# Self-attention stage: the denominators' ones matmuls replaced by sums on GpSimd, with a ring of three banks

## What is computed

```
xn = (x - mu) * rsqrt(var + 1e-5) * gamma + beta       # x: 4 x 512 x 256
q, k = xn @ Wq + bq, xn @ Wk + bk                       # 8 heads of 32
v = xn @ Wv + bv                                        # 8 heads, 256 each
p = softmax(q k^T / sqrt(32))
att = p v
out = att.reshape(S, B, D, H).sum(-1).reshape(B, S, D)  # the sum over H is done on Wv
x = layernorm(x + out)
```

## Time and profile before

| | |
|---|---|
| time, median of 3 runs | 3004.28 us (3003.31 to 3009.35) |
| time of the profiled execution | 3004.98 us |
| its span, first to last instruction | 3002.6 us |
| mean granted clock of TensorE | 0.938 of full speed |
| self-attention stage in the trace | 0 to 276.7 us |
| its windows, first scores to the last | 40.66 to 269.33 us |

### The profile page before, as it was taken

The page is one execution under the profiler, slowest core; times in us unless marked ns, Lnnn a source line. Parts: engine busy times, 40 slices in busy tenths (PEclk is TensorE's granted clock), DMA queues, the critical chain, the costliest instruction groups (busy, mean ns, idle before and its releaser), DMA issues.

```text
span 3002.6 us, 38828 instructions
## 1 busy us (share of the span) xinstructions
PE 2687.5 (90%) x14932; PEld 1683.9 (56%) x14932; DVE 1437.6 (48%) x3277; ACT 1084.5 (36%) x1599; POOL 861.3 (29%) x572
## 2 busy tenths in 40 slices
PE   6788999999999999973999999947899999899997
PEld 3333555555555555542788888825444444368886
DVE  3444555455565555532221221136677767535555
ACT  2433344434444444430221221112276766632111
POOL 4111455555555555554000000042212122110001
PEclk8999999999999999985999999968699999879998
DMA  3101000000000000003444444210000000000000
GB/s 149 37 9 54 12 16 26 16 11 11 31 11 11 16 11 11 6 10 137 156 187 148 170 174 150 107 42 15 24 16 23 20 16 13 12 9 27 22 22 30
DMA packets 58872, 147.88 MB, mean 49 GB/s; under 512 B 18888, under 2 KB 37472, under 8 KB 51904
## 3 DMA queue, kind: packets, MB, share of 16 engines
q1 hardware_dynamic: 52000, 122.72, 11.7%
q0 software_dynamic: 4528, 14.95, 1.5%
q10 hardware_dynamic: 2160, 7.74, 0.7%
HBM read 126.50 MB, written 18.74 MB: 48 GB/s over the span
## 4 chain that ended last, share of the span: by engine, by line
PE 40%; ACT 5%; DVE 3%; issue 2%; POOL 2%; DMA 0%; POOLq 0%; ACTq 0%; DVEq 0%
PE PS L1351 11%; PE PS L1895 6%; PE PS L1362 5%; PE PS L1883 4%; ACT y_P L1069 3%; PE PS L997 3%; PE PS L1014 2%; PE PS L980 2%; DVE y_Mx L1120 1%; POOL l_ga L1826 1%; PE PS L1026 1%; PE PS L1044 1%; PE PS L1682 1%; PE PS L1037 1%; DVE st L110 1%
## 5 line engine op out<-in xcount | busy, mean ns | idle before, releaser
L827 POOL TENSOR_TENSOR x_A<-x_A,x_P 128x1024 f32<-128x1024 f32 x192 | 453.6, 2363 | 221.7 <-ACT x_P L714 207.8
L759 DVE CUSTOM_DVE_ANT_0 x_junk<-PS,x_mb 128x512 bf16<-128x512 f32 x512 | 330.9, 684 | 331.2 <-PE PS L639 330.7
L1120 DVE TENSOR_REDUCE y_Mx<-PS 128x1 f32<-128x512 f32 x512 | 326.1, 684 | 125.0 <-PE PS L1014 123.4
L714 ACT ACTIVATE x_P<-PS,x_kb 128x1024 f32<-128x1024 f32 x256 | 271.6, 1111 | 226.4 <-PE PS L611 224.3
L1351 PE MATMUL PS<-m_xt,m_w 128*128 128x256 f32 x1472 | 326.1, 383 | 19.7 <-issue 18.8
L1351 PEld LDWEIGHTS PS<-m_xt,m_w 128*128 128x128 f32 x1472 | 279.6, 191 | 62.6 <-issue 24.6
L1069 ACT ACTIVATE y_P<-PS 128x1024 f32<-128x1024 f32 x256 | 248.5, 1024 | 128.9 <-PE PS L997 127.4
L624 PE MATMUL PS<-x_P,x_V 128*64 128x512 f32 x1024 | 246.2, 602 | 0.0
L607 PE MATMUL PS<-x_Q,x_K 64*128 64x512 f32 x1536 | 229.5, 403 | 0.0
L1518 DVE SCALAR_TENSOR_TENSOR m_h<-PS,m_fb,m_g 128x256 f32<-128x256 f32 x184 | 89.0, 484 | 265.1 <-ACT m_g L1430 265.1
L1895 PE MATMUL PS<-n_xp,n_wp 128*128 128x512 f32 x816 | 211.4, 408 | 4.3 <-POOL n_wp L2011 4.3
(11 more groups left out here) (283 smaller groups left out, 3831.0 us busy)
## 6 DMA issues: line engine op xcount, KB each, us to landing
m_w<-in_m_w SPq DMA_DIRECT2D x23, 2048.0 KB, 7.9
m_v<-in_m_w SPq DMA_DIRECT2D x23, 1024.0 KB, 9.8
x_w<-in_x_w SPq DMA_DIRECT2D x32, 384.0 KB, 3.0
xs<-zt POOLq DMA_DIRECT2D x16, 368.0 KB, 6.6
m_xb<-xs SPq DMA_DIRECT2D x23, 256.0 KB
ys<-m_yb SPq DMA_DIRECT2D x23, 256.0 KB, 2.2
n_wg<-in_n_w SPq DMA_DIRECT2D x17, 256.0 KB, 2.8
x_cT<-in_ctxT SPq DMA_DIRECT2D x4, 1024.0 KB, 5.5
```

Source lines behind the costliest of these rows:

```text
L714: act.e.activation(Pt[gt % 6][:], PS[:, 2 * i:2 * i + 2, :], ACT.Exp, bias=kb[u // 8 % 2][:, kt:kt + 1], scale=scale).then_inc(s["exp"], 1)
L759: dve.e.tensor_tensor_reduce(junk[j % 2][:], ring.bank("max", v, j), mb[b % 2][:, half * 512:half * 512 + 512], 1.0, -3e38, ALU.add, ALU.m ...
L827: pool.e.tensor_tensor(A[u % 2][:], Pt[(gt - 1) % 6][:] if kt == 1 else A[u % 2][:], Pt[gt % 6][:], ALU.add).then_inc(s["add"], 1)
L1120: dve.e.tensor_reduce(Mx[v % 2][:, h, qt, half:half + 1], ring.bank("max", v, j), AX.X, ALU.max).then_inc(s["red"], 1)
```

## The change

GpSimd sums the four tiles of probabilities of a unit into two new tiles `a_A` (two heads each), by six additions of 128x1024 elements in a unit; the addition for window t stands in POOL's list ahead of the side jobs of window t+1. The ones matmuls of `pv` go; in their place stands one group of four ones matmuls in a unit, `den`, on `a_A`, in window t = 1 of the next unit. Exp waits until the additions have read the tile of `a_P` that it overwrites. The chain of the denominators, the multiplication and all that follows (`den`, `rec`, `mul`, `ot`, `st`, `nr`, `tp`) is placed anew, `mul` a unit later. Bank 5 joins the ring. The list of windows ends with (8, 3) instead of (8, 1).

```
-            ring = Turns(one_bank[6:8])
-            ob = one_bank[4:6]
+            ring = Turns(one_bank[5:8])
+            ob = one_bank[4]
             at = {
-                0: [("tp", -3, 0), ("k", 2, 0), ("max", 1, 2), ("pv", 0, 0), ("ev", -1, 0), ("max", 1, 3), ("ot", -2, 0), ("ot", -2, 1)],
-                1: [("tp", -3, 1), ("q", 2, 0), ("max", 1, 4), ("pv", 0, 1), ("max", 1, 5), ("ot", -2, 2), ("ot", -2, 3)],
-                2: [("v", 2, 0), ("max", 1, 6), ("pv", 0, 2), ("max", 1, 7), ("rec", -1, 0), ("st", -2, 0)],
-                3: [("turn", 1, 0), ("max", 2, 0), ("pv", 0, 3), ("max", 2, 1), ("mul", -1, 0), ("nr", -2, 0)],
+                0: [("k", 2, 0), ("max", 1, 2), ("pv", 0, 0), ("ev", -1, 0), ("max", 1, 3), ("st", -3, 0)],
+                1: [("q", 2, 0), ("max", 1, 4), ("den", -1, 0), ("pv", 0, 1), ("mul", -2, 0), ("max", 1, 5), ("nr", -3, 0)],
+                2: [("tp", -3, 0), ("v", 2, 0), ("max", 1, 6), ("pv", 0, 2), ("max", 1, 7), ("ot", -2, 0), ("ot", -2, 1)],
+                3: [("tp", -3, 1), ("turn", 1, 0), ("max", 2, 0), ("pv", 0, 3), ("max", 2, 1), ("rec", -1, 0), ("ot", -2, 2),
+                    ("ot", -2, 3)],
             }
...
-                return [(-1, 0)] + [(u, t) for u in range(n) for t in range(T)] + [(n, 0), (n, 1)]
+                return [(-1, 0)] + [(u, t) for u in range(n) for t in range(T)] + [(n, t) for t in range(T)]
...
-                for part in range(2):
-                    for h in range(4):
-                        pe.wait_ge(s["exp"], 2 * gt + h // 2 + 1)
-                        w = onef[:] if part else V[v % 3][:, kt, head(h)]
-                        m = pe.e.matmul(ob[part][head(h), :], w, Pt[(2 * gt + h // 2) % 6][:, h % 2, :], start=kt == 0, stop=kt == T - 1)
+                for h in range(4):
+                    pe.wait_ge(s["exp"], 2 * gt + h // 2 + 1)
+                    m = pe.e.matmul(ob[head(h), :], V[v % 3][:, kt, head(h)], Pt[(2 * gt + h // 2) % 6][:, h % 2, :],
+                                    start=kt == 0, stop=kt == T - 1)
...
+            def adds(gt, pp):
+                gt = max(gt, gt // T * T + 1)
+                return 6 * (gt // T) + 2 * (gt % T - 1) + pp + 1
...
+                        elif name == "den":
+                            bank = take(pe, "den", v, j)
+                            pe.wait_ge(s["one"], 2)
+                            pe.wait_ge(s["add"], 6 * (v + 1))
+                            for h in range(4):
+                                m = pe.e.matmul(bank[head(h), :], onef[:], A[h // 2][:, h % 2, :], start=True, stop=True)
+                            m.then_inc(s["den"], 1)
...
                         for pp in range(2):
+                            act.wait_ge(s["add"], adds(gt - 3, pp) if gt >= 3 else 0)
                             act.e.activation(Pt[(2 * gt + pp) % 6][:], PS[:, 2 * pp:2 * pp + 2, :], ACT.Exp,
...
+                            act.e.activation(E[v % 2][0][:], ob, ACT.Copy).then_inc(s["ev"], 1)
+                        elif name == "den":
+                            act.wait_ge(s["den"], v + 1)
                             act.wait_ge(s[f"den{v % 2}"], 16 * (v // 2))
-                            for part in (1, 0):
-                                act.e.activation(E[v % 2][part][:], ob[part], ACT.Copy).then_inc(s["ev"], 1)
+                            act.e.activation(E[v % 2][1][:], ring.bank("den", v, j), ACT.Copy).then_inc(s["dev"], 1)
...
                 for u, t in windows():
+                    gt = u * T + t - 1
+                    if 0 < gt < n * T and gt % T > 0:
+                        for pp in range(2):
+                            cur = Pt[(2 * gt + pp) % 6]
+                            pool.wait_ge(s["exp"], 2 * gt + pp + 1)
+                            pool.wait_ge(s["den"], gt // T)
+                            pool.wait_ge(s["add"], adds(gt - 1, pp) if gt % T > 1 else 0)
+                            pool.e.tensor_tensor(A[pp][:], Pt[(2 * gt + pp - 2) % 6][:] if gt % T == 1 else A[pp][:], cur[:],
+                                                 ALU.add).then_inc(s["add"], 1)
                     for name, v, j in side(u, t):
```

More of the change, by code:

```diff
@@ L174, in l0_attention @@
             n, T, NBK, scale = 8, 4, 3, 32 ** -0.5
-            s = stage_sems(c, 0, "a", "proj hi cf lo vm vc max red turn nm score exp pv ev rec mul ob res one pad sum qk wv bv zt "
+            s = stage_sems(c, 0, "a", "proj hi cf lo vm vc max red turn nm score exp pv ev dev add den rec mul ob res one pad sum qk wv bv zt "
                                       "den0 den1 dc0 dc1 dr0 dr1 rb0 rb1")
@@ L190, in l0_attention @@
             Pt = [sbuf(c, f"a_P{i}", [P, 2, S]) for i in range(6)]
+            A = [sbuf(c, f"a_A{i}", [P, 2, S]) for i in range(2)]
             E = [[sbuf(c, f"a_E0{j}", [P, S]) for j in range(2)], [ax["E0"], ax["E1"]]]
@@ L234, in l0_attention @@
                 for name, v, i in side(u, t):
-                    if name in ("turn", "k", "q", "v", "ot"):
+                    if name in ("turn", "k", "q", "v", "den", "ot"):
                         ring.add(name, v, i)
@@ L251, in take @@
                         pe.wait_ge(s["vc"], v + 1)
+                    elif name == "den":
+                        pe.wait_ge(s["dev"], v + 1)
                     elif name == "ot":
@@ L281, in values @@
                 if kt == 0:
-                    pe.wait_ge(s["ev"], 2 * v)
+                    pe.wait_ge(s["ev"], v)
                     pe.wait_ge(s["vc"], v + 1)
-                for part in range(2):
-                    for h in range(4):
-                        pe.wait_ge(s["exp"], 2 * gt + h // 2 + 1)
-                        w = onef[:] if part else V[v % 3][:, kt, head(h)]
-                        m = pe.e.matmul(ob[part][head(h), :], w, Pt[(2 * gt + h // 2) % 6][:, h % 2, :], start=kt == 0, stop=kt == T - 1)
+                for h in range(4):
+                    pe.wait_ge(s["exp"], 2 * gt + h // 2 + 1)
+                    m = pe.e.matmul(ob[head(h), :], V[v % 3][:, kt, head(h)], Pt[(2 * gt + h // 2) % 6][:, h % 2, :],
+                                    start=kt == 0, stop=kt == T - 1)
                 m.then_inc(s["pv"], 1)
+            def adds(gt, pp):
+                gt = max(gt, gt // T * T + 1)
+                return 6 * (gt // T) + 2 * (gt % T - 1) + pp + 1
             def pe_prog(pe):
@@ L433, in pool_prog @@
                             pool.wait_ge(s[f"rb{v % 2}"], 16 * 4 * (v // 2 + 1))
-                            pool.wait_ge(s["ev"], 2 * (v + 1))
+                            pool.wait_ge(s["ev"], v + 1)
                             pool.wait_ge(s["ob"], 4 * (v // 2 - 1))
@@ L464, in sp_prog @@
                     for name, v, j in side(u, t):
-                        if name == "ev" and v < n - 1:
-                            sp.wait_ge(s["ev"], 2 * v + 1)
+                        if name == "den" and v < n - 1:
+                            sp.wait_ge(s["dev"], v + 1)
                             sp.wait_ge(s[f"dc{v % 2}"], 16 * (v // 2))
```

## The result

The changed kernel takes 3023.65 us (median, 3013.40 to 3026.22), the kernel before 3005.36 beside it: a ratio of 1.0052 (95% interval 1.0033 to 1.0071), slower. Four of its six executions took 3021.5 to 3026.2 us and two 3013.4 and 3015.0, so the medians differ by 18.3 us and the means, from which the ratio comes, by 15.6. The forecast was 3018. The profiled execution took 3025.77 us, its span is 3024.0, 21.4 more than before, at a mean granted clock of 0.929 (0.938).

The account below looks back on a forecast made before the run. In the first stage, PE work ahead of the second `max` lengthens each window, since PE's next scores wait for DVE's reduction. Gains 23.6 and losses 36.8 us give +13.2 on 3004.98, so 3018 us; range 3000 to 3029.

Parts of the forecast that it names:

- (a): Window (1, 1): `nr0` of batch 2 waits for a late `rstd` behind POOL's additions and `zeros`; loss 8.7 us.
- (b): Window (2, 2): `nr0` of batch 3 waits for `rstd` behind additions, then norms run beside more additions; loss 8.4 us.
- (c): Window (4, 2): `nr` at the end of t = 1 meets POOL's additions, delaying reductions; loss 4.0 to 6.2, taken as 5.1 us.
- (d): Window (6, 2): same norms beside additions, with less in POOL's queue; window 10.2 against 7.1 us, loss 3.1 us.
- Step (1): Windows without ones groups: second `max` comes 0.97 us earlier; 2.83 us a unit for units 0 to 5, 2.3 for unit 6.
- (f): TensorE's clock falls after the idle times of PE in (a), (b) and (e); loss 5 us.
- Step (2): Ring of three banks removes PE's waits for ACT in (1, 2) and (2, 3); gain 3.9 us.
- Step (3): `tp` moves to t = 2 and 3, partly hidden behind Exp; gain 0.4 us.
- (e): End of the stage, from scores of (7, 0): POOL's last additions, then `rstd`, norms and `tp`; loss 6.5 us.
- R1: Rival: norms pass between POOL's additions in (1, 1), (2, 2), (4, 2), (6, 2); faster, 2997 us; chance 0.12.
- R2: Rival: clock stays low after every stall, 15.3 or 20.4 us instead of 5; 3028 to 3033 us; chance 0.12.
- R3: Rival: POOL is not late at all, only the end costs; 17 us gained, 2987 us; chance 0.03.

Follow-up runs that it names:

- e8: Changed kernel with `zeros` in (3, 0), `nr` heading t = 1, batch 3's input norms in (2, 1), four of the last unit's six additions back on PE: 2995.47 us.
- e9: Kernel before plus only POOL's 48 additions, sums unused, and Exp's wait for them; ones groups, job places and ring of two kept: 3026.61 us, ratio 1.0072.
- e2: Changed kernel with the stage's four norms per batch on ACT instead of DVE, POOL working out the bias: 2997.51 us, ratio 0.9975.
- e4: Changed kernel with POOL's `zeros` memset and 16 DMA issues moved from window (0, 3) to the end of (3, 0): 3013.74 us, ratio 1.0027.
- e7: Changed kernel with four of the last unit's six additions left to PE as ones matmuls: 3020.09 us, ratio 1.0046.
- e5: Changed kernel with `rstd` of window (2, 2) put ahead of the pair of additions that stood before it: 3020.70 us, ratio 1.0055.
- e3: Changed kernel with POOL's additions cut to 16 of 512 columns, denominators left out, same instructions and order: 2994.56 us, ratio 0.9962.
- e11: Changed kernel with norms on ACT, `zeros` in window (3, 0) and the last unit's sums on PE: 2991.70 us, ratio 0.9954.
- e12: e8 plus unused ones matmuls on PE at the end of windows without `ot`, and three such groups before the last `tp`: 2987.21 us, ratio 0.9936.

## Why the prediction was right, step by step

The stage grew by 12.5 us in the profile (forecast 13.2). The mechanism was right for the three large stalls of (a), (b) and (c), but that the sum came so close is in part luck: (d) did not happen, (c) was larger, and the clock did more on both sides than the forecast had. The terms follow, with what they measured. For a window whose clock was low, its length at full clock is taken from another kernel that has it: (2, 3) 5.93 and (1, 2) 7.2 from e8, (6, 2) 6.44, (0, 1) 8.94 and (0, 2) 7.21 of the old kind from e9; (6, 1) and (6, 3) from the kernel before.

- **Step (1), the ones groups.** Right. 6.30, 6.36 and 5.82 instead of 7.16, 7.35 and 6.67 for t = 0, 2 and 3: 2.70 a unit (forecast 2.83). V's group alone takes 1.00 us between the two `max`, where the earlier trace rows leave 0.88 for it. Unit 6 gave 0.9, in (6, 0), instead of 2.3. (6, 2) and (6, 3) never ran wholly at full clock without ones groups and are taken at their old lengths, so what they may have gained is set against the clock in (f). 16.9 in all, forecast 19.3.
- **Step (2), the ring.** Right, 4.2 instead of 3.9. (1, 2) went from 11.80 to 7.2 and (2, 3) from 9.00 to 5.93, 7.7 in all. 2.1 + 2.1 of it lie ahead of the job that had to wait, 1.9 are step (1), and 1.6 are the clock: behind its wait the old kernel ran (1, 2) partly at the low level (granted 0.86; V's projection took 2.49 us, in e8 1.95). The probabilities times V, in the kernel before and in e8 at full clock:

```profile
100.84 1.89 PE L288 MATMUL PS<-a_P,a_V 128*32 128x512 f32 x8
...
91.26 1.07 PE L291 MATMUL PS<-a_P,a_V 128*32 128x512 f32 x8
```

- **Step (3)**, `tp`: 0.8 gained in (4, 0) and (4, 1), 0.4 given back in (4, 2), which takes 6.75 us in e2 and e8 where (5, 2) takes 6.36. 0.4, as forecast.
- **Step (a), (1, 1).** 8.9, forecast 8.7; `rstd` ended at 89.2, forecast 89.4, norms done at 95.6, forecast 96.0. e4 confirms it. The size is that of one course of the race: e7 has the same code and 8.75 us in this window, after three windows at a lower clock. What a low clock costs just ahead of the stall comes off the stall, and the forecast counted the two apart.
- **Step (b), (2, 2).** 7.9, forecast 8.4; e5 shows that the norms' pace and not the order sets it.
- **Step (c), (4, 2).** 6.3, just above the 4.0 to 6.2 given. The first norm did not slip in ahead: recorded from 193.29 beside an addition from 193.30, it lasted 2.53 us.
- **Step (d), (6, 2).** Wrong. The norms took 2.35 us, as POOL had but one instruction left, and were done at 254.54, before PE's first `max` of the window at 255.53, which waited for ACT. They cost nothing; the forecast had its queue fuller than it was.
- **Step (e), the end.** 6.9, forecast 6.5, and the queue of POOL did end the stage. But without the additions 4.1 would have been lost all the same (e3, e7), by `ot`, statistics and norms two windows later, which the forecast did not price; shortening the queue alone gets back 2.7.
- **Step (f), the clock.** 4.0 net in the windows, forecast 5, and this agreement is luck. Low were (1, 2), (2, 0), (2, 1), (2, 3) and (3, 0), 1.7 + 2.8 + 1.6 + 2.2 + 1.6, after the stalls as expected, and (6, 1) to (6, 3), 2.3 + 1.5 + 1.9, with no stall ahead of them: 15.6. Before, it was (0, 1), (0, 2), (4, 3), (5, 0) and (6, 2) with 10.0, and (1, 2) with 1.6. The forecast priced only the falls after stalls, at 5; they cost 9.9. It had neither unit 6, 5.7, nor that 11.6 us of the old falls would go.

Gains 16.9 + 4.2 + 0.4 = 21.5 (forecast 23.6), losses 8.9 + 7.9 + 6.3 + 6.9 + 4.0 = 34.0 (36.8). What the forecast did not have at all lies outside the stage: 2.1 us before (0, 0) and 6.9 after it, both with unchanged work. Of the latter some 4 are a cross-attention that starts at a lower clock:

```profile
276.70:312.30 35.60, 30.62 (x135) 16.68 (x137) 18.61 (x49) 6.57 (x11) 2.65 (x6) 0.90 0.29 101
...
291.00:331.00 40.00, 35.71 (x135) 19.44 (x137) 18.43 (x49) 6.79 (x12) 2.64 (x6) 0.76 0.26 87
```

The first row is before, the second the changed kernel: the same 135 matmuls in 35.6 and 40 us. The rest is within what that part varies by. R1, norms let through between additions, is refuted by e5 and e9. R2, a clock that stays low after every stall, did not come about in that form, but after (a) and (b) the clock took 9.9 us in the stage, twice the 5 of the forecast, and some 4 behind the end. R3 and R4 needed a POOL that is not late or stalls half as dear, and neither was so.

## What to carry to other kernels

When work goes to an idle engine, look not only at whether it keeps up but at what the long instructions do to short ones: those of the same queue that others wait for, and those of another engine that are held up beside them. Here three groups of norms, late or held up, cost 23 us where 192 matmuls less gave 17, and another place or another engine for them was the main part of what turned +0.5% into -0.3% and -0.5%. After a stage has been shortened, look at the gaps that are left on PE: here filling them with useless work was worth 8 us. And before a difference in one window is put down to an edit, look whether the engine came to it at the same time: a stall behind another engine's queue shrinks by what was lost ahead of it.

## What the runs showed of the hardware

Four VectorE norms of 128x256 took 1.38 us with POOL idle and 2.25 beside one instruction of 128x512, but 9.39 (e5) and 9.60 us (changed) beside a full queue of additions. POOL was slowed little: a pair of additions took 4.73 and 4.76 us instead of 4.69, an instruction of 128x512 in e4 1.49 instead of 1.27. ScalarE was not slowed (2.06 and 2.08 us for four norms beside additions, 2.07 with POOL idle, in e2).
The Trainium skill, "SBUF — State Buffer", section "Who interferes with whom", lets the later of the two engines wait for the holder's whole instruction, and the trace agrees for VectorE; that only one norm got in between two instructions of POOL while its queue was full is more than the section says.

TensorE's clock fell to its 1.2 GHz level in (6, 1) of the changed kernel, and in e8 and e11 too. In the changed kernel no gap of units 5 and 6 ahead of it was longer than 1.42 us; PE stops once or twice a window there and was busy for 74% from 232 to 240 us. In e8 (2, 0), (3, 0), (3, 1), (4, 3) and (5, 0) were lengthened too; in e12, which fills the last gap of many windows, these five have their full speed lengths (6.30, 6.30, 7.15, 5.82 and 6.30 us).
The Trainium skill, "TensorE: Matmul & The Clock Gate", section "A second HAM failure mode: psum-queue depth-cycling", describes a clock that swings when PE pauses briefly but often between groups; e12, which only fills such pauses, agrees by its 8 us. Which pauses decide was not separated.
